# Two attention layers in one software pipeline: a fourth pair buffer, other slots for the small products, and the turned tile's steps moved later

## The reference

```python
# layer 0, per image: x is 128 x 1024
t = W_theta x + b_theta; p = W_phi x + b_phi            # 64 x 1024 each
f = softmax(t^T p / 8)                                   # 1024 x 1024
x = x + W_fuse (f applied to x) + b_fuse
# layer 1
h = group_norm(x, 32 groups) * gn_w + gn_b
q, k, v = q_w h + q_b, k_w h + k_b, v_w h + v_b          # 128 x 1024 each
a = softmax(q^T k / sqrt(128))
y = x + p_w (a applied to v) + p_b
```

## Time and profile before

| | |
|---|---|
| runs: median (lowest to highest) | 1895.29 us (1894.0 to 1898.93) |
| the profiled execution's own time | 1903.5 us |
| its span, first to last instruction | 1901.7 us |
| granted TensorE clock, mean | 0.99 |
| PE busy | 1759.0 us (92%) |
| PE weight loads busy | 1191.6 us (63%) |
| VectorE (DVE) busy | 1432.4 us (75%) |
| ScalarE (ACT) busy | 1441.4 us (76%) |
| GpSimd (POOL) busy | 1273.3 us (67%) |
| transposes by DMA (`et<-pair`) | 384, median 4.6 us from issue to landing |

### The profile page before, as it was taken

How to read it: one execution, slowest core, us unless ns; L and a number is a source line. 1 busy time by engine, 2 the same in 40 slices (tenths; PEclk the granted TensorE clock), 3 DMA queues, 4 the chain that set the end, 5 groups by cost and what they waited for, 6 DMA issues and landing times.

```text
span 1901.7 us, 34446 instructions
## 1 busy us (share of the span) xinstructions
PE 1759.0 (92%) x8966; PEld 1191.6 (63%) x8966; DVE 1432.4 (75%) x1650; ACT 1441.4 (76%) x2152; POOL 1273.3 (67%) x1321
## 2 busy tenths in 40 slices
PE   4799999999999999999999999999999999999986
PEld 2466666666666666666666666666666666666654
DVE  4577778778777787777787777877777878777854
ACT  3577877777877777877877877877887877877854
POOL 2566776666776666776666776666776666776652
PEclk9899999999999999999999999999999999999998
DMA  3578777877878778778777778778777777778764
GB/s 77 101 144 151 158 151 165 160 150 157 163 145 172 157 151 160 158 150 169 151 156 158 156 155 170 146 160 159 149 162 164 153 156 157 148 157 168 140 126 95
DMA packets 860085, 286.33 MB, mean 151 GB/s; under 512 B 822304, under 2 KB 823200, under 8 KB 860064
## 3 DMA queue, kind: packets, MB, share of 16 engines
q1 hardware_dynamic: 860064, 286.08, 74.4%
HBM read 50.86 MB, written 17.04 MB: 36 GB/s over the span
## 4 chain that ended last, share of the span: by engine, by line
issue 24%; DVE 17%; DMA 16%; ACT 14%; PE 11%; POOL 9%; SPq 9%; DVEq 1%; ACTq 0%; POOLq 0%
DMA et<-pair 11%; SPq L340 7%; DVE neg_max L704 6%; PE o_ps L416 5%; DMA rden_dram<-rden 4%; ACT s_ps L610 3%; ACT pair L635 3%; DVE pair L721 3%; DVE phi L795 2%; PE s_ps L416 2%; PE s_ps L454 2%; DVE x L758 2%; ACT et L620 2%; DVE x_max L781 2%; PE m_ps L416 1%
## 5 line engine op out<-in xcount | busy, mean ns | idle before, releaser
L416 PE MATMUL o_ps<-et,v_hi 128*128 128x512 f16 x2048 | 699.0, 383 | 50.3 <-DVE x L758 31.2
L704 DVE TENSOR_REDUCE neg_max<-s_ps 128x1 f32<-128x1024 f32 x512 | 624.4, 1220 | 66.0 <-PE s_ps L416 56.0
L416 PEld LDWEIGHTS o_ps<-et,v_hi 128*128 128x128 f16 x2048 | 203.0, 99 | 303.4 <-issue 119.8
L416 PE MATMUL o_ps<-et,v_lo 128*128 128x512 f16 x1024 | 390.6, 381 | 0.0
L721 DVE SCALAR_TENSOR_TENSOR pair<-s_ps,pair 128x1024 f16<-128x1024 f32 x256 | 312.1, 1219 | 75.6 <-ACT pair L635 74.4
L416 PE MATMUL s_ps<-phi,theta 128*128 128x512 f32 x1024 | 331.1, 446 | 6.0 <-ACT e_copied L610 3.7
L610 ACT ACTIVATE s_ps<-s_ps,neg_max 128x1024 f32<-128x1024 f32 x256 | 277.3, 1083 | 58.5 <-DVE neg_max L704 57.8
L846 POOL TENSOR_TENSOR pair<-e_copied,pair 128x1024 f16<-128x1024 f32 x128 | 274.6, 2145 | 23.3 <-ACT pair L633 23.3
L715 DVE SCALAR_TENSOR_TENSOR et<-s_ps,et 128x1024 f16<-128x1024 f32 x128 | 156.7, 1224 | 170.5 <-ACT et L620 170.5
L935 POOL TENSOR_TENSOR x<-x,xr 128x512 f32<-128x512 f32 x64 | 81.5, 1274 | 288.0 <-DVE x L758 288.0
L635 ACT ACTIVATE pair<-s_ps 128x1024 f16<-128x1024 f32 x256 | 262.2, 1024 | 8.1
(11 more groups left out here) (113 smaller groups left out, 3076.9 us busy)
## 6 DMA issues: line engine op xcount, KB each, us to landing
rden_row<-rden_dram SPq DMA_DIRECT2D x128, 256.0 KB, 3.9
xs<-in_x SPq DMA_DIRECT2D x32, 512.0 KB, 4.0
phi<-phi SPq DMA_DIRECT2D x64, 256.0 KB, 3.2
out_y<-y_sb SPq DMA_DIRECT2D x64, 256.0 KB, 2.5
et<-pair SPq DMA_TRANSPOSE x384, 4.6
rden_dram<-rden SPq DMA_DIRECT2D x128, 2.0 KB, 1.5
w_f<-in_w_fuse_t SPq DMA_DIRECT2D x1, 64.0 KB, 3.1
ident_sb<-in_ident SPq DMA_DIRECT2D x1, 64.0 KB, 2.3
```

The costliest lines, as they stand in the source:

```text
L416: mm = pe.matmul(out, lhs_t, rhs, start=start and n == 0, stop=stop and n == len(terms) - 1)
L704: nc.vector.tensor_reduce(neg_max[:, t % 4:t % 4 + 1], s_ps[:, part(t), :], AX.X, ALU.max, negate=True).then_inc(s_max, 1)
```

## The change

1. `pair` gets a fourth buffer (`PAIRS = 4`). The new function `place` sends the copied tile to buffer 0 and buffer 3 in turn.
2. The units stand in other slots: `q1` and `w0` swap (slots 8 and 7), `mx` moves from slot 14 to 11, `v0` from 15 to 14.
3. GpSimd makes the first half of `h_lo` in slot 2, ahead of the copied tile's low half, and the second in slot 3. The waits for `h` and `h_hi` are written so that they also hold in slot 2.
4. TensorE makes the transposes of the turned tile behind the value quarter of the slot, not ahead of it.
5. ScalarE takes the high half of the turned tile behind the next tile's exponential, not ahead of it.
6. VectorE takes the low half of the turned tile a slot later (`t = s - 3`), between `maxima` and `normalised`.

```diff
-PAIRS = 3
+PAIRS = 4
-UNITS = {0: "gn1", 1: "gn2", 2: "v1", 4: "k0", 5: "k1", 6: "q0", 7: "q1", 8: "w0", 9: "w1", 10: "tp0", 12: "tp1",
-         14: "mx", 15: "v0"}
+UNITS = {0: "gn1", 1: "gn2", 2: "v1", 4: "k0", 5: "k1", 6: "q0", 7: "w0", 8: "q1", 9: "w1", 10: "tp0", 11: "mx",
+         12: "tp1", 14: "v0"}
-H_LO_SLOTS = (3, 4)
+H_LO_SLOTS = (2, 3)
+    def place(s):
+
+        return PAIRS - 1 if s % GROUP == COPIED and s // GROUP % 2 else s % GROUP
...
                     scores(it, s, 0)
                     scores(it, s, 1)
                     unit(it, s)
+                    values(it, s)
                     transposes(it, s)
-                    values(it, s)
...
                 for s in range(SLOTS):
+                    exponentials(it, s)
                     turned_hi(it, s)
-                    exponentials(it, s)
                     pair_hi(it, s)
...
-            def take_lo(it, s):
-                t = s - 2
-                if not here(tile_at, it, t) or here(copied_at, it, t):
-                    return
-                r = t % GROUP
+            def turned_lo(it, s):
+                t = s - 3
                 if here(turned_at, it, t):
...
+            def pair_lo(it, s):
+                t = s - 2
...
                     maxima(it, s)
+                    turned_lo(it, s)
                     normalised(it, s)
-                    take_lo(it, s)
+                    pair_lo(it, s)
...
-                    pool.wait_ge(s_h32, before(h_at, it, s))
-                    pool.wait_ge(s_hhi, before(h_at, it, s))
+                    pool.wait_ge(s_h32, before(h_at, it, H_SLOT) + 1)
+                    pool.wait_ge(s_hhi, before(h_at, it, H_SLOT) + 1)
```

More of the change, by code:

```diff
@@ L45 @@
 NORM_MAX = 64.0
-UNITS = {0: "gn1", 1: "gn2", 2: "v1", 4: "k0", 5: "k1", 6: "q0", 7: "q1", 8: "w0", 9: "w1", 10: "tp0", 12: "tp1",
-         14: "mx", 15: "v0"}
-STAGE = {"v1": 0, "k0": 1, "k1": 0, "q0": 1, "q1": 0, "w0": 1, "w1": 0, "v0": 1}
+UNITS = {0: "gn1", 1: "gn2", 2: "v1", 4: "k0", 5: "k1", 6: "q0", 7: "w0", 8: "q1", 9: "w1", 10: "tp0", 11: "mx",
+         12: "tp1", 14: "v0"}
+STAGE = {"v1": 0, "k0": 1, "k1": 0, "q0": 1, "w0": 0, "q1": 1, "w1": 0, "v0": 1}
 SPLIT_LAG = {"v1": 2, "k0": 1, "k1": 1, "q0": 1, "q1": 1, "w0": 1, "w1": 2, "v0": 1}
@@ L159, in until_part_before @@
         return value(lambda i: count(kind, 0, (part_before(i, s) or 0) + 1), it)
+    def place(s):
+        return PAIRS - 1 if s % GROUP == COPIED and s // GROUP % 2 else s % GROUP
     def same_pair(s):
-        return lambda g: int(tile_at(g) and g % GROUP == s % GROUP)
+        return lambda g: int(tile_at(g) and g % GROUP != TURNED and place(g) == place(s))
     def same_group(s):
@@ L340, in move @@
                 sp.dma_start_transpose(et[:, t // GROUP % 4, r, :, :],
-                                       pair[:, r, :, :].rearrange("q a n -> q (a n)")).then_inc(s_pair_t[r], 16)
+                                       pair[:, place(t), :, :].rearrange("q a n -> q (a n)")).then_inc(
+                                           s_pair_t[place(t)], 16)
             def reciprocals_out(it, s):
@@ L435, in scores @@
                     if s == PHASE + GROUP:
-                        pe.wait_ge(s_split, before(staged_at, it, 8))
+                        pe.wait_ge(s_split, before(staged_at, it, 9))
                 out = s_ps[:, part(s), half * HALF:(half + 1) * HALF]
@@ L463, in values @@
                 if quarter == 0:
-                    for r in range(PAIRS):
-                        pe.wait_ge(s_pair_t[r], 16 * before(same_pair(r), it, first + GROUP))
+                    for t in range(first, first + TURNED):
+                        pe.wait_ge(s_pair_t[place(t)], 16 * before(same_pair(t), it, first + GROUP))
                     pe.wait_ge(s_tlo, before(turned_at, it, first + GROUP))
@@ L627, in pair_hi @@
                     return
-                n, r = before(tile_at, it, t), t % GROUP
+                n, r = before(tile_at, it, t), place(t)
                 act.wait_ge(s_exp, n + 1)
@@ L718, in take_lo @@
                                                    op0=ALU.mult, op1=ALU.subtract).then_inc(s_tlo, 1)
+            def pair_lo(it, s):
+                t = s - 2
+                if not here(crossed_at, it, t):
                     return
+                r = t % GROUP
                 dve.wait_ge(s_pair_hi, before(crossed_at, it, t) + 1)
@@ L925, in copied_lo @@
                         pool.wait_ge(s_copied_hi, before(copied_at, it, t) + 1)
-                        rest(pair[:, COPIED, 1, :], e_copied[:, :], pair[:, COPIED, 0, :], s_copied)
+                        rest(pair[:, place(t), 1, :], e_copied[:, :], pair[:, place(t), 0, :], s_copied)
             def outputs(it, s):
```

## The result

Nine runs of the changed kernel gave a median of 1903.43 us (1898.69 to 1908.45), nine of the kernel before 1896.98 us. The ratio is 1.0036, 95% interval [1.0023, 1.0049]: 0.36% slower, where 1848 us and a gain of 2.5% were forecast. The profiled execution took 1898.69 us (span 1896.9), clock 0.99 as before. It is the fastest of the nine, and so shows about as much time as the kernel before, not the loss: what follows explains where the forecast gain went.

A forecast was written before the change was run, and what follows sets the result against it. TensorE, 92% busy, was taken to bound the kernel through its stops. Stretches of 21.75, 29.41 and 3.80 us made a step of 54.96 us against 56.48; 31 steps save 47 us, giving 1848 us, range 1804 to 1888.

The forecast's parts named there:

- Which stops go: TensorE's five stops a step vanish: two turned-tile transposes, the value product of slot 14, units k0 and q0; 3.35 us together.
- S(0) to V(6) holds what TensorE gains: Slot 0's scores to slot 6's value product: of 1.56 us removed stops nothing is left; 21.75 us against 21.48.
- Tile 1 is issued at 937.7: In the chain into slot 6's value product, tile 1's DMA transpose leaves at 937.7, against 937.40 before.
- mx stays within the stretch: Between the value products of slots 6 and 14, moving mx leaves the stretch's length alone; mx itself takes 0.2 us.
- V(6) to V(14): Slot 6's to slot 14's value product: 29.91 us less 1.79 of stops plus 1.29 for v0, 29.41 us.
- V(14) to S(0): Slot 14's value product to slot 0's scores: 5.09 us less v0, which moved out, 3.80 us.
- the reason why edit 1 is worth having at all: Without the buffer wait tile 9's chain starts about 0.5 us earlier; otherwise slot 14's value product would wait 0.34 us.
- The copied tile's slack of 1.1 us: GpSimd's low half of copied tile 0 has 1.1 us to spare before it delays slot 6's value product.
- The rivals: Shorter chain into V(6) 0.14, 1802 us; VectorE limit 0.20, 1873; copied tile holding SP queue 0.08, 1917; no change 0.08, 1895.
- No change: Rival, chance 0.08: chains into value products of slots 2, 6, 14 start late by what TensorE gained; 1895 us.
- the lower bound of 0.6 us a step: Smallest gain a step: both moves on VectorE cost their full 1.14 us, less 0.2 for what is hidden.
- the 56 that were to make the whole reading wrong: Sign in the profile: a step staying above 56 us makes the whole reading wrong; about 55 us was right.

The follow-up runs named there:

- e4: Changed kernel with the image load in slot 4 of the SP queue instead of slot 1; ratio to the kernel before 0.9918.
- f2: Changed kernel with the units q1, w0, mx and v0 back in their old slots; ratio to the kernel before 0.9926.
- g3: Kernel before with the fourth pair buffer and nothing else; ratio to the kernel before 0.9873.
- f3: Changed kernel with three pair buffers as before; ratio to the kernel before 1.0230.
- e3: Changed kernel with the transposes ahead of the load of the reciprocals' row in the SP queue; ratio to the kernel before 1.0076.
- k2: Kernel before with the fourth pair buffer and all three moves of the turned tile (points 4 to 6); ratio to the kernel before 0.9883.
- k3: Kernel before with the fourth pair buffer and the image load in slot 4 of the SP queue; ratio to the kernel before 0.9869.
- g1: Changed kernel with the units in their old slots and the image load in slot 4; ratio to the kernel before 0.9917.
- g4: Changed kernel with units and h_lo halves in old slots, image load in slot 4, SP transposes ahead of the reciprocals' row load; ratio to before 0.9949.
- k4: Kernel before with the fourth pair buffer and the SP transposes ahead of the reciprocals' row load; ratio to the kernel before 0.9870.
- e1: Changed kernel with the unit mx in slot 13 instead of 11; ratio to the kernel before 1.0099.

## Why the prediction was wrong

- *Which stops go*: right. T(11), T(15), V(14), `k0`, `q0` all went, and ScalarE's wait for the buffer.
- *S(0) to V(6) holds what TensorE gains*: right in kind, wrong in size. Forecast 21.75 us, measured 22.71 over 30 steps (21.86 before). The step that failed is "Tile 1 is issued at 937.7", half a us behind its low half. It was issued 2.3 us behind it (994.63 to 996.91), because SP stood before the row load and that before the small store behind the image load. The chain that I wrote down left out the SP queue's other DMAs; the step that I read in the kernel before showed the tile leaving 0.5 us behind its low half, and I took that as a property of the queue. That step was not typical: the mean there was 1.0 us, and 1.8 in the changed kernel. Up to the low half the chain was right: 0.24 us later behind S(0) on average, 0.27 forecast. e4, which moves the image load and no other instruction, gives 1.2%.
- *"mx stays within the stretch"*: this is the step that failed worst. I counted `mx` at its own 0.2 us. It moved right behind `tp0`, whose result VectorE must read out of the one `m_ps` first, and that wait of 1.1 us lies in the TensorE part, where nothing hides it. V(6) to V(14): forecast 29.41, measured 30.27 as a mean. The last transpose for V(14) landed 24.7 us behind S(8), 25.0 forecast, so V(14) would have been just in time without the stop. f2 prices the units' new slots at 21 us (1.1%). The wait stands in the code ahead of every unit.
- *V(14) to S(0)*: forecast 3.80 us, measured 3.81 in the step shown.
- *"the reason why edit 1 is worth having at all"*: too small. The buffer alone is worth 1.3% on the kernel before (g3) and 1.9% within the change (f3).
- *The copied tile's slack of 1.1 us*: held; it counted only when e3 brought tile 1 forward.
- *The rivals*: none of the four was it. "No change" came nearest in time (0.08), but not by its reason. V(14) waited for nothing, and the stretches did change: S(0) to V(6) grew by 0.85 us and V(6) to V(14) by 0.3 over the means before, V(14) to S(0) fell by 1.28. The loss of the units was in no case.
- *The bounds and the signs*: the lower bound of 0.6 us a step does not follow from what stands beside it (3.35 less 1.56 less twice 1.14 plus 0.2 is below zero). Steps of 56.8 us are above the 56 that were to make the whole reading wrong; of its parts, the list of stops that go held all the same.

In sum, a step of 54.96 us was forecast; the profile's mean is 56.79 (30 steps; 56.92 before), and the runs show no gain at all. The 1.83 us are 0.96 in S(0) to V(6), tile 1's late issue and what else delays V(6), and 0.86 in V(6) to V(14), which is the 1.1 us before `mx` less 0.25 for a stop before `tp0` that I had not listed and that went as well. The one step that I read was also 0.44 us shorter than the mean of its kernel. Against g3 one can say it shorter: the buffer gives 1.3%, the units take 1.1%, and the turned tile's moves, worth 0.6% in their company, give nothing without them. The 0.4% that are left, between k2 and f2, are not in the steps.

Why so many edits moved the two parts against each other (f2, k2, k3) is not settled. A full DMA queue from slot 10 to slot 6 would do it, and V(14) points there: with the units in their old slots and four buffers it waits 1.2 to 1.7 us a step for the transposes on average (f2, g1, g3, g4, k2 to k4, some of it for `normalised`). But no run took transfers away.

## What to carry to other kernels

When a unit of work is moved, list the waits that its code makes at the new place, not only the ones that it had: a wait for a shared buffer that was long over in the old slot can be the longest of the new one. For a transfer near the limit, read what stands ahead of it in its queue and what each of those waits for; its distance from its producer in one trace is no constant. And time each part of a bundle alone: here one line of it was worth more than the whole.

## What the hardware showed that I had not expected

A VectorE operation of four columns took 1.05 us instead of 0.22 when it started while GpSimd was at work. GpSimd in e1, beside the VectorE rows shown there:

```profile
984.06 1.27 POOL L944 TENSOR_TENSOR x<-x,xr 128x512 f32<-128x512 f32 x1 [7.05 <-DVE x L766]
```

It ends at 985.33; `den_scaled`, started at 984.30, ends at 985.35. Of the 128 `den_scaled` in e1, 63 started inside a GpSimd operation. 56 of them took over 0.4 us, most ending 0.01 to 0.02 us behind it; the other 7 started in its last 0.35 us. None of the 65 others took so long. In the changed kernel it starts 0.17 us ahead of that operation in slot 14 and takes 0.22 us. The Trainium skill ("SBUF — State Buffer", section SBUF: two separate sides) says that a VectorE operation with two SBUF inputs and a GpSimd operation that reads SBUF exclude each other for the whole instruction; these rows agree, `den_scaled` reads `den` and `e_factors` from SBUF. So a tiny operation can cost a whole GpSimd operation, and in e1 it did so in the loop.
